# Weight splits at other places in a hand-written step order, and one more round in the loop, of a macaron transformer kernel

## The reference, cut to what matters

```
x = x + 0.5 * ffn(layernorm(x))          # "call 0"
x = x + attn(layernorm(x)) @ weight      # global attention, 16 heads
x = x + 0.5 * ffn(layernorm(x))          # "call 1", same weights again

ffn, for each of 2 layers:
    q, k, v = split(shift_token(x) @ wqkv)          # 8 heads of 64
    q, k = rotary(l2norm(q) * q_scale, l2norm(k) * k_scale)
    x = x + local_attention(q, k, v) @ wo           # blocks of 128, own and previous block
    h = layernorm(shift_token(x)) * ln_g + ln_b
    a, g = split(h @ w1 + b1)
    x = x + (a * gelu(g)) @ w2 + b2
```

## Time and profile before

| | us |
|---|---|
| median of 3 runs | 3964.91 |
| lowest, highest | 3960.32, 3965.76 |
| the profiled execution's own time | 3964.91 |
| its span, first to last instruction | 3963.2 |
| PE busy | 3751.8 (95%) |
| DVE, ACT, POOL busy | 2647.8, 2237.6, 2191.9 |
| mean granted TensorE clock | 0.985 |

### The profile page before, as it was taken

How to read it: one execution, slowest core, us unless ns; L and a number is a source line. 1 busy time by engine, 2 the same in 40 slices (tenths; PEclk the granted TensorE clock), 3 DMA queues, 4 the chain that set the end, 5 groups by cost and what they waited for, 6 DMA issues and landing times.

```text
span 3963.2 us, 75451 instructions
## 1 busy us (share of the span) xinstructions
PE 3751.8 (95%) x23552; PEld 3070.4 (77%) x23552; DVE 2647.8 (67%) x7286; ACT 2237.6 (56%) x5232; POOL 2191.9 (55%) x2179
## 2 busy tenths in 40 slices
PE   3999999999999799999999999998999999999997
PEld 2777777777777688888888888886777777777776
DVE  6677777777777455555555555656777777767774
ACT  2666665567656455444444444445756765567564
POOL 3465565555555355555555655654555555555553
PEclk9999999999999899999999999999999999999999
DMA  4000001110100100000000010001010011100110
GB/s 142 16 31 28 19 19 54 47 36 24 33 28 29 46 27 22 1 17 7 12 17 2 17 44 1 17 1 51 20 33 24 19 41 50 38 31 24 34 32 25
DMA packets 119061, 114.72 MB, mean 29 GB/s; under 512 B 13180, under 2 KB 116232, under 8 KB 118792
## 3 DMA queue, kind: packets, MB, share of 16 engines
q1 hardware_dynamic: 118792, 111.44, 8.9%
HBM read 73.69 MB, written 29.36 MB: 26 GB/s over the span
## 4 chain that ended last, share of the span: by engine, by line
PE 86%; DVE 6%; issue 3%; ACT 2%; POOL 2%; DMA 1%; DVEq 0%; SPq 0%; ACTq 0%; POOLq 0%
PE psum L1363 21%; PE psum L1364 20%; PE psum L1365 20%; PE psum L1477 6%; PE psum L1487 5%; PE psum L1507 4%; PE psum L1612 3%; PE psum L1466 3%; PE psum L1560 1%; DVE probs L1065 1%; PE psum L1443 1%; PE psum L1424 1%; DVE nT_lo L1124 1%; DVE turned_sin L1031 1%; DVE ssq L1038 1%
## 5 line engine op out<-in xcount | busy, mean ns | idle before, releaser
L685 POOL TENSOR_TENSOR ge_lo<-ge,ge_hi 128x512 fp32r<-128x512 f32 x512 | 716.5, 1402 | 543.7 <-PE psum L1365 311.8
L885 ACT ACTIVATE ge<-psum 128x512 f32<-128x512 f32 x512 | 306.4, 598 | 626.3 <-PE psum L1612 621.7
L645 POOL TENSOR_SCALAR probs<-probs,rz 128x256 f32<-128x256 f32 (+1 forms) x1024 | 446.1, 456 | 354.7 <-DVE rz L1079 354.7
L1253 DVE CAST ge_hi<-ge 128x512 fp32r<-128x512 f32 x512 | 245.8, 481 | 540.1 <-ACT ge L885 536.1
L791 ACT ACTIVATE probs<-probs,nb,rq 128x256 f32<-128x256 f32 (+1 forms) x1024 | 575.0, 565 | 20.8 <-DVE nb L1073 17.8
L1065 DVE CUSTOM_DVE_ANT_0 probs<-psum,mask 128x256 f32<-128x256 f32 (+1 forms) x1024 | 339.2, 387 | 251.4 <-PE psum L1477 198.2
L627 POOL TENSOR_TENSOR rinv<-ssq,minus_half 128x16 f32<-128x16 f32 x124 | 376.1, 3033 | 126.6 <-DVE ssq L1042 123.2
L655 POOL TENSOR_TENSOR hid_lo<-gate,hid_hi 128x512 fp32r<-128x512 f32 x160 | 208.1, 1301 | 320.7 <-ACT hid_hi L823 320.7
L1363 PE MATMUL psum<-wqkv_hi,hT_hi 128*128 128x512 f32 x768 | 318.1, 414 | 5.7 <-DVE hT_lo L1016 3.4
L772 ACT ACTIVATE squares<-psum 128x512 f32<-128x512 f32 x256 | 153.2, 599 | 286.0 <-PE psum L1365 268.1
L622 POOL TENSOR_TENSOR turned_qk<-turned_qk,turned_sin 128x512 f32<-128x512 f32 x128 | 165.1, 1289 | 258.3 <-DVE turned_sin L1031 258.1
(11 more groups left out here) (163 smaller groups left out, 10650.8 us busy)
## 6 DMA issues: line engine op xcount, KB each, us to landing
xnext<-stream SPq DMA_DIRECT2D x32, 512.0 KB, 4.4
xmid<-stream SPq DMA_DIRECT2D x32, 512.0 KB, 3.8
stream<-xmid SPq DMA_DIRECT2D x16, 512.0 KB, 2.9
nrm<-xmid SPq DMA_DIRECT2D x32, 224.0 KB
wbuf<-L_ffn_wqkv SPq DMA_DIRECT2D x8, 768.0 KB, 8.3
wbuf<-L_ffn_w SPq DMA_DIRECT2D x8, 682.0 KB, 4.2
x_all<-L_attn_x SPq DMA_DIRECT2D x8, 512.0 KB, 7.5
stream<-x_all SPq DMA_DIRECT2D x8, 512.0 KB, 3.9
```

The costliest lines, as they stand in the source:

```text
L645: last = nc.gpsimd.tensor_scalar(pu, pu, rz[:, h, t:t + 1], 1.0, ALU.mult, ALU.mult)
L685: nc.gpsimd.tensor_tensor(ges[1][:, k % 4, :], ge[:, k % 4, :], f32(ges[0][:, k % 4, :]), ALU.subtract).then_inc(S["g_lo"], 1)
L885: nc.scalar.activation(ge[:, k % 4, :], RB[k % 2], ACT.Exp, scale=GSCALE, accum_out=gz[:, h, t:t + 1]).then_inc(S["g_exp"], 1)
L1253: V.tensor_copy(ges[0][:, k % 4, :], ge[:, k % 4, :]).then_inc(S["g_hi"], 1)
```

## The change

Three things change. In the list of DVE, `i0` and `R0` are swapped; `f0` moves from behind `+c1` to directly behind `P2`; `f2` moves from the end of the list to a place ahead of `+ss3` and `+c2`. In the list of ACT, `f0` moves ahead of `H7`. And round 2 of each call (rounds 2 and 18), written out before, becomes the first iteration of the loop that follows.

```diff
-ACT_STEPS ... +sq1 O2 H7 f0 +sq2 O3 f1 ...
+ACT_STEPS ... +sq1 O2 f0 H7 +sq2 O3 f1 ...

-DVE_STEPS ... X1 X2 R0 i0 -y3 R1 R2 ... P2 +rq1 L7 +c0 +c1 f0 P3 f1 +rq2 x l B +rk2
-              +ss2 r +rk3 +rq3 j0 j1 nl0 nl1 +ss3 +c2 f2
+DVE_STEPS ... X1 X2 i0 R0 -y3 R1 R2 ... P2 f0 +rq1 L7 +c0 +c1 P3 f1 +rq2 x l B +rk2
+              +ss2 r +rk3 +rq3 j0 j1 nl0 nl1 f2 +ss3 +c2

         a_round(n0, prev=False, load=2 * call)
         a_round(n0 + 1)
-        a_round(n0 + 2)
-        with eng.Fori(0, B - 4) as j:
-            a_round(n0 + 3 + j)
+        with eng.Fori(0, B - 3) as j:
+            a_round(n0 + 2 + j)
         a_round(n0 + B - 1, switch=2 * call + 1)
```

More of the change, by code:

```diff
@@ L47 @@
 ACT_STEPS = ("-G2 -G3 E0 -u2 E1 i0 E2 i2 H0 -G4 -u3 H1 E3 i1 -u4 H2 E4 E5 H3 O0 E6 O1 H4 E7 +zh0 +zh1 -G5 H5 +sq0 "
-             "-u5 +sk0 +sk1 H6 +sq1 O2 H7 f0 +sq2 O3 f1 +Kc0 +Qc0 +sk2 +sk3 +vh0 +sq3 +Qc1 +Qc2 +vh1 +vh2 +Kc1 nh0 "
+             "-u5 +sk0 +sk1 H6 +sq1 O2 f0 H7 +sq2 O3 f1 +Kc0 +Qc0 +sk2 +sk3 +vh0 +sq3 +Qc1 +Qc2 +vh1 +vh2 +Kc1 nh0 "
              "nh1 G0 f2 u0 G1 +Qc3 +vh3 +Kc2 +Kc3 u1").split()
-DVE_STEPS = ("-y0 c3 Y -y1 X0 -y2 X1 X2 R0 i0 -y3 R1 R2 L0 X3 i2 L1 -y4 X4 i1 L2 R3 X5 R4 X6 L3 P0 R5 X7 L4 P1 R6 "
-             "+zl0 R7 +zl1 -y5 L5 +rq0 +rk0 +ss0 -F -e L6 +rk1 +ss1 P2 +rq1 L7 +c0 +c1 f0 P3 f1 +rq2 x l B +rk2 "
-             "+ss2 r +rk3 +rq3 j0 j1 nl0 nl1 +ss3 +c2 f2").split()
+DVE_STEPS = ("-y0 c3 Y -y1 X0 -y2 X1 X2 i0 R0 -y3 R1 R2 L0 X3 i2 L1 -y4 X4 i1 L2 R3 X5 R4 X6 L3 P0 R5 X7 L4 P1 R6 "
+             "+zl0 R7 +zl1 -y5 L5 +rq0 +rk0 +ss0 -F -e L6 +rk1 +ss1 P2 f0 +rq1 L7 +c0 +c1 P3 f1 +rq2 x l B +rk2 "
+             "+ss2 r +rk3 +rq3 j0 j1 nl0 nl1 f2 +ss3 +c2").split()
 POOL_STEPS = ("-ul1 -ul2 N0 N1 N2 N3 -ul3 N4 -ul4 N5 N6 N7 -ul5 +b0 +d0 +p0 +p1 +d1 +b1 +d2 +b2 s +d3 +b3 +p2 +p3 "
```

## The result

| | before | after |
|---|---|---|
| median, us | 3962.61 | 4013.59 |
| lowest, highest | 3960.19, 3965.76 | 4007.13, 4016.35 |
| runs | 4 | 4 |
| the profiled execution's own time | 3964.91 | 4006.17 |
| its span | 3963.2 | 4004.4 |

The changed kernel is slower: ratio 1.0126, interval 1.0108 to 1.0143, or +51 us between the medians. I had forecast +18.4 us, and the time is far above the range. The two profiled executions differ by 41.2 us of span.

A forecast was written before the change was run, and what follows sets the result against it. The prediction took PE, busy 95% of the span, plus its stalls to bound the kernel. It summed 3.4 + 3.2 + 8.0 + 0.8 + 3.0 = +18.4 us on 3964.91 to 3983.3 us, range 3972 to 3996.

The forecast's parts named there:

- part 4: Rounds 2 and 18 into the loop: one more looped iteration costs 0.4 us per call, +0.8 us in all.
- Part 3 (f2): Four load rounds, f2 ahead of +ss3 and +c2: -y0 late, so PE's a1 2.0 us late each, +8.0 us.
- f2's delay is hidden: Rival, chance 0.06: PE has other work at a1, so f2's later place costs nothing there; sum +7.4 us, 3972.3 us.
- Part 2 (f0): Four load rounds, f0 behind P2: PE's stall moves from W3 to A7, 0.8 us each, +3.2 us (1.2 to 5.6).
- f0's stall simply goes: Rival, chance 0.08: waits before W3, some 7.1 us, are won and none comes; sum +8.1 us, 3973.0 us.
- Part 1 (i0): Two switch rounds, i0 ahead of R0: POOL's N0 ends 1.7 us later, all paid for lack of slack, +3.4 us.
- Part 5 (the clock): Load rounds: a 1.2 GHz stretch behind each new 3.5 us stall, 0.75 us each, +3.0 us.
- The bound of +13: Upper clock bound: step B of round 0 at 8.90 us (+4.1), six lengthened stalls at twice 0.75 us each (+9).
- the low clock spreads: Rival, chance 0.15: upper bound for f0's move and 8 us instead of 3 for the clock; sum +26, 3991 us.
- B at full clock in round 8: Sign of being wrong: PE's step B in load round 8 running at 2.4 GHz instead of 1.2 GHz.
- the -8 of the rival: Rival, chance 0.12: step B of rounds 8 and 24 runs at 2.4 GHz, -8.2 us for +3.0; sum +7.2, 3972.1 us.

The follow-up runs named there:

- the orders: Kernel before with only the new places of i0, f0 and f2, rounds 2 and 18 still written out: 3986.66 us against 3959.56, ratio 1.0068.
- the fold: Kernel before with only rounds 2 and 18 moved into the loop, all step lists as before: 3981.43 us against 3959.56, ratio 1.0053.
- three singles: Kernel before with only f2, only f0 or only i0 moved, one kernel each: 3970.68, 3969.80 and 3964.34 us against 3957.85.
- i0 alone: Kernel before with only i0 and R0 swapped in DVE's list: 3964.34 us against 3957.85, ratio 1.0014.

## Why the prediction was wrong

**The sign was right, and what failed is part 4.** I priced "rounds 2 and 18 into the loop" by the length of a round in and out of the loop, and gave it 0.8 us. Rounds 2 and 18 themselves bear that out within 0.7 us (77.07 and 77.44 against 76.88 and 77.48), and rounds 3 and 19 behind them add 1.8 us. But the price treats code as if it had no place. Taking a written-out round away moves all that comes behind it in DVE's program, and a loop that begins 540 us behind the second fold came to lie where each jump back waits 4 us for its instructions. Measured: +21.9 us, of which some 16 are the place of that loop (rounds 26 to 30 are 17.4 us longer), and some 6 lie at the jumps of the attention loop. With the last loop out of the slow place (the changed kernel with 16 idle instructions) the loss is 32 us: 14 more than the forecast of 18.4, where the changed kernel is 33 over it. Those 32 us are near the orders' 27.1 and the fold's other 6.

**Part 3 (f2): the stall was sized right, its place was not.** Four stalls, +7.4 us by the waits against the 8.0 forecast. PE stops at `+K2` for 3.4 us and not at `a1`, though the prediction has both waits in one stall. The rival "f2's delay is hidden" falls.

**Part 2 (f0): the upper end.** I took 0.8 us per round, the middle of 0.3 and 1.4, "since f0 is already running when +d1 arrives". The waits give +5.8 us over four rounds, just over the upper end of 5.6. By the rule that I cited from the Trainium skill's "SBUF — State Buffer", section "Who interferes with whom", it would be that end (5.6), and the trace shows its pattern: f0 2.77 us instead of 1.76, `+d1` 2.08 instead of 1.29. The rival "f0's stall simply goes" falls; it goes with P3 ahead of f0.

**Part 1 (i0).** N0 ends 1.65 us later against its round's start (650.22 + 5.06 / 3 = 651.91, an estimate as N1 and N2 stand in the same row; less 613.71 it is 38.20; before, 643.53 - 606.98 = 36.55), for the 1.7 forecast. T0's waits grow by 2.8 us in two rounds, but those for L1084 shrink by 1.0, so the waits grow by 1.8 us for the 3.4: the chain had some slack, which the prediction denied. Round 7 is 1.43 and round 23 is 2.45 us longer in the changed kernel.

**Part 5 (the clock): mis-sized.** 3.0 us for the whole. The three singles are 16 us longer than their waits, all three together some 12 us, both with the uncertainty given above. I had taken the 0.75 us by which round 7 and its twin differ; with i0 alone PE's busy time there grew by 1.4 and 2.3 us, since both now fall to the low level for longer. The bound of +13 holds the 12.

**Between the rivals.** The orders alone gave +27.1 us, for which I had 17.6 (the sum without the fold), 25 by "the low clock spreads". B at full clock in round 8, which I had named as a sign of being wrong, did come: B takes 4.92 us in rounds 8 and 24 of the changed kernel, where it took 8.90 and 8.92, and that is the -8 of the rival. It is in part luck. In round 8 of the kernels with the order of before in the load rounds, B takes 8.9 us in four profiles and 4.8 to 5.2 in three, and in the changed kernel with 16 idle instructions it takes 6.95. And rounds 9 and 25 are only 1.8 and 1.1 us shorter for it, as the stall at `+K2` and the slower matmuls behind it lie in the same windows; and rounds 1 and 17, where there was little to give back (B in 4.79 and 6.54 us before, 5.11 and 7.01 after), are 4.1 and 5.8 us longer. No rival had the fold in it.

## What to carry to other kernels

An edit that adds or removes instructions moves every loop behind it. After each edit, look at the jumps back of the loops on every engine, and at the instruction loads inside them, before a difference is put down to the edit itself. In a kernel bound by PE, price a stall by its wait and the slower matmuls that may follow it: here the times rose by more than the waits, by up to as much again. Before a split is moved to another chain, try to swap it with its neighbour: P3 ahead of f0 was the one change of order here that won.

## What the runs showed of the hardware

- A loop of 269 DVE instructions jumps back in 0.3 us or in 3.5 to 5 us, by its place in the program: slow at 74, 76 and 204 instructions from a fast place, fast at 2, 60, 90 and 92. Slow iterations load five blocks of 8192 bytes, fast ones none. By the lines of 256 instructions in the Trainium skill's "Advanced Engine Details and Errata", section "ISA Cache", 204 would lie outside the slow place; it lies inside (jumps of 3.7 to 4.1 us), so the measurement decides.
- A DVE loop too long for this pays at every place tried: the attention loop has 878 DVE instructions, and its two jumps take 2.8 to 3.8 us in all kernels (from the jump's record to the next register instruction), the one before included (3.36 and 3.42).
- PE's own instructions can come late too: 1.6 to 2.7 us behind each jump back of the attention loop in the five kernels with the fold, and at most 0.4 us in the nine others.
- With 76 idle instructions PE waits 1.80 to 2.02 us for the gate in each of the five slow iterations. A stretch at 1.2 GHz stands behind four of these waits (windows at 0.98) and none behind the first (1.85 us, 1.00). With the fold alone the longest wait, 2.72 us, has none behind it and three of 1.80 to 1.94 us have one. So the clock's answer did not follow the length of the stall. In the changed kernel the three longer waits (2.67 to 2.93 us) have such a stretch and the two shorter ones (1.54 and 1.64 us) have none.
